# Second edge stage of a two-layer graph network: one-hot joins and accumulating scatters, or edges sorted by source with a scan and plain scatters

## Chip, cores and metric

One core of a Trainium2 chip. The metric is the device time of one execution in microseconds, of which the median over the runs is given. Everything is float32.

## The reference, cut to what matters

There are N = 100000 nodes with 64 features and E = 50000 edges (src, dst, weight), which come sorted by dst.

```python
# layer 0
agg = segment_sum(x[src] * w[:, None], dst, N)
out = leaky(x * agg @ W1 + b1) + leaky(agg @ W2 + b2)
x = layernorm(x + out * rsqrt(max(sum(out*out), 1e-12)))
# layer 1: the neighbour is dst, the sum goes to src
msg = gelu(gelu(x[dst] @ W1p + b1p) @ W2p + b2p) * w[:, None]
agg = segment_sum(msg, src, N)
h = gelu(gelu(concat(x, agg) @ W1u + b1u) @ W2u + b2u)
x = layernorm(x + h * rsqrt(max(sum(h*h), 1e-12)))
```

## The kernel before, in words

Three stages follow each other, with a barrier of all engines between them. Nodes go in 98 chunks of 1024 (128 partitions x 8), edges in 98 windows of 512 (4 tiles of 128).

**Stage one, `first_edges`.** For each window POOL gathers x[src] by four indirect DMAs (`gather`, L247) into xg, 120 of them ahead. PE spreads the window's 512 dst keys along the free axis (`spread_rows`, L292), DVE compares them with each tile's own keys, which gives matrices of 128 x 128 to 128 x 512 with the edge weight where the keys agree (`equal_rows`, L372, tile `weigh`), and counts with a second pass which edge of a run comes first (L378, tile `seen`). PE multiplies the matrices with the gathered rows (`join`, L304), so that one row of each run holds the run's sum; ACT copies it out (`take`, L327); POOL scatters the four tiles with accumulation into `table` in DRAM (`scatter`, L260), rows that are no run's sum going to spare rows. POOL issues a window's scatters only after those of the window before have landed. The first scatter is plain (bypass), and waits until `table` has been cleared, 25 transfers on SP's queue. Beside it SP loads chunks of x (`load_x`), DVE and ACT centre and copy them (`build`, L355 and L358; `copy_x`), and SP stores them next to the sums. DVE, PE and ACT work through a list `order` written out by hand, in which the entries (0, k) are the work above. The entries (1, k) do the same comparison for the second list of keys (src, with the edges still in order of dst): PE spreads, DVE compares and counts, and `store_join` on ACT's queue writes the window's matrices (640 KB) to `joins` in DRAM.

**Stage two, `second_edges`,** is a software pipeline of ROUNDS = NWIN + 6 rounds. In round t an engine does parts of windows t, t-1, ..., t-5, in the order written in its loop. One window is 12 blocks of 128 rows, 4 gathered for the edges (POOL, `gather`, L538, from `table` by dst) and 8 of the chunk (SP, `load`). Layer 0 is finished for all 12 (`box` is the input of a window, `y` its result), and layer 1's message is computed for the 4 edge blocks. The names of the steps, in the order of the engines' loops:

- PE: `products(t-2, 2)` (L588), `join(t-5)` (L634), `turn_neighbours(t-4)` (L607), `outputs(t-2, 0)` and `outputs(t-2, 1)` (L598, 12 matmul records each, one half of the bank pair o_p each), `first_product` (L614), `turn` and `products` 0 and 1 (L579, L588), `second_product(t-4)` (L619 bias, L621).
- ACT: `second_gelu` (L702), `slope(t-2, 2)` (L676), `take(t-5)` (L709), `square_centred` (L687), `neighbours_in`, `square(t-2)` (L682, from o_p to sq_o), then `evict` (L670), `first_gelu` and `slope` 0 and 1.
- DVE: `sum_outputs(t-2)` (L767), `roots` (L775 to L787, ten linked small operations), a copy of the root into the spare end of o_p (L789), `leak(t-1, 0)` (L758), `normalize(t-3)` (L806), `scale(t-2)` (L793, in place in PSUM), `leak` 1, `add_rows(t-2)` (L801), `leak` 2, three `multiply(t)` (L750), `sum_centred(t-2)` (L763).
- POOL: four scatters (L557, accumulating, into `state` by src), then the next gathers: on the average 359 / 91 a round.

The output block o_p is read last by `add_rows`, and `outputs(i, 0)` waits for `added` of the window before, for `squared` of it, and for `leak(i, 2)`. `join` multiplies the stored matrices, which SP loads (`load_join`, 640 KB), with the messages g2.

**Stage three, `last_rows`,** turns the node rows of `state` into the output.

## Time and profile before

| | |
|---|---|
| median of 3 runs | 2925.66 us (2924.0 to 2927.83) |
| the profiled execution, its own time | 2925.36 us |
| its span, first to last instruction | 2923.6 us |
| stage one, stage two, stage three | 0 to 1257, 1257 to 2539, 2539 to 2924 us |
| busy share of the span | POOL 80%, DVE 76%, PE 73%, ACT 36% |
| mean granted TensorE clock | 0.769 of full |

The span is a little shorter than the execution's time, since what lies ahead of the first instruction and behind the last is not in it. Engines run beside each other, so a busy share says how much an engine has to do, and an engine's idle time, with what ended it, says what it waited for. An operation that a row calls "issue" was waiting for nothing that the profile shows. A duration in a group is a mean; consecutive operations of one engine overlap by some hundredths of a microsecond.

### The profile page before, as it was taken

Reading aid. Unit: us, or ns where it says so; the run is one execution under the profiler, and the core shown is the slowest. Engines: PE = TensorE matmul, PEld = TensorE weight load, DVE = VectorE, ACT = ScalarE, POOL = GpSimd, SP = SyncE. Lnnn points to the kernel's source line nnn. Section 1 sums busy time; section 2 is a strip of 40 time slices with the busy share of each in tenths; the row PEclk is TensorE's granted clock in tenths of the full one; section 3 lists DMA queues with packets and bytes.
Section 4 is the critical chain, followed back from the end, with each engine's and each line's share of the span. In section 5 each row is a group of like instructions: output and inputs, shape, how many; then the busy total and the mean of one; then the engine's idle time right before and its main releaser. Section 6 shows DMA issues by size and latency. Waiting matters only on the chain. (4 is left out here: it accounts for less than half of the span.)

```text
span 2923.6 us, 40992 instructions
## 1 busy us (share of the span) xinstructions
PE 2133.4 (73%) x12594; PEld 1674.9 (57%) x12594; DVE 2219.9 (76%) x5824; ACT 1060.2 (36%) x1964; POOL 2327.0 (80%) x1770
## 2 busy tenths in 40 slices
PE   3036555555555553369999999999998999699997
PEld 3035555555555543347777777777776666466664
DVE  5069988888888886547788777777777777278998
ACT  0000000000000000035555555545554555289997
POOL 7777888888888888758878888888888887479998
PEclk8555555555555555579999999999999999699998
DMA  9889888888888767568777777777776776456664
GB/s 227 214 197 200 178 177 180 175 178 183 180 183 172 160 142 155 96 163 183 185 185 184 180 167 181 181 169 175 179 181 157 184 172 149 89 173 219 222 219 169
DMA packets 1035280, 516.39 MB, mean 177 GB/s; under 512 B 539713, under 2 KB 997489, under 8 KB 1035065
## 3 DMA queue, kind: packets, MB, share of 16 engines
q1 hardware_dynamic: 764616, 372.57, 48.1%
q0 software_dynamic: 143440, 76.97, 19.0%
q10 hardware_dynamic: 127008, 64.23, 7.6%
q8 instruction: 104, 1.70, 0.3%
q14 instruction: 112, 0.91, 0.1%
HBM read 269.84 MB, written 243.78 MB: 176 GB/s over the span
## 5 line engine op out<-in xcount | busy, mean ns | idle before, releaser
L304 PE MATMUL sums<-xg,weigh 128*128 128x64 f32 x1960 | 431.8, 416 | 518.2 <-ACT ms L327 350.9
L557 POOL DMA_INDIRECT state<-ms,sidx x391 | 621.5, 1590 | 147.4 <-issue 117.4
L304 PEld LDWEIGHTS sums<-xg,weigh 128*128 128x128 f32 x1960 | 417.6, 325 | 551.2 <-issue 474.9
L260 POOL DMA_INDIRECT table<-ms,sidx x391 | 615.7, 1575 | 136.1 <-issue 114.7
L372 DVE TENSOR_SCALAR weigh<-rowp,key,ew 128x128 f32<-128x128 f32 (+3 forms) x784 | 424.2, 604 | 162.8 <-PE rowp L292 155.4
L538 POOL DMA_INDIRECT box<-table,node_dst x391 | 385.8, 987 | 126.6 <-issue 111.2
L247 POOL DMA_INDIRECT xg<-in_x,node_src x391 | 380.8, 974 | 120.7 <-issue 107.1
L327 ACT ACTIVATE ms<-sums 128x256 f32<-128x256 f32 x98 | 37.6, 384 | 1137.9 <-DMA table<-ms,sidx 996.8
L378 DVE SCALAR_TENSOR_TENSOR seen<-rowp,key,earlier 128x128 f32<-128x128 f32 (+3 forms) x784 | 383.6, 546 | 0.0
L588 PE MATMUL z_p<-turned_s,wz 128*128 128x512 f32 x588 | 326.9, 639 | 22.7 <-ACT turned_s L670 21.0
L598 PE MATMUL o_p<-cenz,leaky 128*128 128x65 f32 x2352 | 302.1, 288 | 42.0 <-DVE leaky L758 41.9
L598 PEld LDWEIGHTS o_p<-cenz,leaky 128*128 128x128 f32 x2352 | 289.4, 203 | 62.8 <-DVE leaky L758 62.7
L292 PE MATMUL rowp<-ident,key 128*128 128x128 f32 x784 | 183.7, 413 | 130.1 <-DVE seen L378 123.1
L634 PEld LDWEIGHTS ffo<-g,weigh_in 128*128 128x128 f32 x1960 | 239.8, 196 | 48.1 <-issue 47.7
L676 ACT ACTIVATE leaky<-z_p,bz 128x512 f32<-128x512 f32 x294 | 202.0, 687 | 126.1 <-PE z_p L588 114.5
L767 DVE TENSOR_REDUCE v<-sq_o 128x12 f32<-128x780 f32 x98 | 94.6, 966 | 192.3 <-ACT sq_o L682 192.3
L292 PEld LDWEIGHTS rowp<-ident,key 128*128 128x128 f32 x784 | 164.4, 238 | 130.9 <-DVE seen L378 123.9
L634 PE MATMUL ffo<-g,weigh_in 128*128 128x64 f32 x1960 | 235.9, 277 | 1.6 <-issue 1.6
L758 DVE SCALAR_TENSOR_TENSOR leaky<-z_p,bz,leaky 128x512 f32<-128x512 f32 x294 | 218.5, 743 | 18.7 <-ACT leaky L676 9.1
L892 POOL TENSOR_TENSOR inv<-ssq,mhalf 128x8 f32<-128x8 f32 x98 | 161.0, 1642 | 59.1 <-DVE ssq L1004 59.1
L579 PEld LDWEIGHTS turned_p<-ident,box 128*128 128x128 f32 x1176 | 155.4, 153 | 84.6 <-issue 66.9
L670 ACT ACTIVATE turned_s<-turned_p 128x512 f32<-128x512 f32 x294 | 174.7, 595 | 47.4 <-PE turned_p L579 39.6
(97 smaller groups left out, 3555.2 us busy)
## 6 DMA issues: line engine op xcount, KB each, us to landing
box<-table SPq DMA_DIRECT2D x97, 768.0 KB, 5.2
joins<-weigh ACTq DMA_DIRECT2D x98, 640.0 KB, 3.8
weigh_in<-joins SPq DMA_DIRECT2D x98, 640.0 KB, 7.1
table<-rows SPq DMA_DIRECT2D x97, 512.0 KB, 5.3
pair<-state SPq DMA_DIRECT2D x97, 512.0 KB, 4.0
xin<-in_x SPq DMA_DIRECT2D x97, 256.0 KB, 6.1
state<-y SPq DMA_DIRECT2D x97, 256.0 KB, 7.5
out<-y SPq DMA_DIRECT2D x97, 256.0 KB, 2.2
```

The lines of the kernel that those rows point to most:

```text
L247: pool.indirect_dma_start(out=xg[:, i, :], out_offset=None, in_=x[:, :], in_offset=bass.IndirectOffsetOnAxis(ap=node[0][:, i:i + 1], axis= ...
L260: pool.indirect_dma_start(out=table[:, :], out_offset=bass.IndirectOffsetOnAxis(ap=sidx[0][:, i:i + 1], axis=0), in_=ms[k % MR][:, b, :], ...
L292: last = pe.transpose(rowp[n][k % 2][:, b * P:(b + 1) * P], key[n][:, i:i + 1].to_broadcast([P, P]), ident[:, :])
L304: last = pe.matmul(sums[k % 2][:, a * D:(a + 1) * D], block_of(0, k, b)[:, a * P:(a + 1) * P], xg[:, k * WT + b, :], start=b == a, stop=b ...
L372: last = dve.tensor_scalar(block_of(n, k, b), rowp[n][k % 2][:, (b + 1 - m) * P:(b + 1) * P], key[n][:, i:i + 1], ew[:, i:i + 1], ALU.is_e ...
L378: last = dve.scalar_tensor_tensor(out=seen[b][:, 0:m * P], in0=rowp[n][k % 2][:, (b + 1 - m) * P:(b + 1) * P], scalar=key[n][:, i:i + 1], ...
L538: pool.indirect_dma_start(out=box[i % SB][:, b, :, :].rearrange("p a f -> p (a f)"), out_offset=None, in_=table_rows[:, :], in_offset=bass ...
L557: pool.indirect_dma_start(out=state[:, :], out_offset=bass.IndirectOffsetOnAxis(ap=sidx[1][:, at:at + 1], axis=0), in_=ms[k % SM][:, b, :] ...
L588: pe.matmul(z_p[n % 2][:, :], wz[:, :], turned_s[q][:, :], start=True, stop=True).then_inc(z_up, 1)
L598: last = pe.matmul(o_p[:, b, g * M8:(g + 1) * M8], leaky[i % 2][r // 4][:, r % 4 * P:(r % 4 + 1) * P], cenz[:, :], start=True, stop=True)
L634: last = pe.matmul(ffo[:, (WT + a) * D:(WT + a + 1) * D], weigh[i % SW][:, at * P:(at + 1) * P], g2[i % 2][:, b * D:(b + 1) * D], start=b ...
L758: dve.scalar_tensor_tensor(out=leaky[i % 2][q][:, :], in0=z_p[n % 2][:, :], scalar=bz[:, 0:1], in1=leaky[i % 2][q][:, :], op0=ALU.add, op1 ...
```

## The change

Stage one no longer builds the second list's matrices. `equal_rows` becomes `weigh_rows` and `count_rows`, for the first list alone. Instead, the edges (src, dst, weight, as three float arrays `edges` of 128 x 512) are sorted by src with a bitonic network: 136 compare-and-swap steps, 16 changes of sign of a part of the keys, and 14 turns, which exchange the partition and the free axis by transposes on PE and copies on ACT. In a swap ACT copies the lower half of each pair aside (`keep_lower`), DVE compares the two halves' keys into a mask in PSUM, and makes two predicated copies. The 166 steps are spread over the windows: 12 each in windows 0 to 3, the others up to window 83. Then DVE marks which edge has the key of the one before and which ends a run, PE and ACT turn the lists once more, and the flags and the sorted weights (`runs`, 2 x 256 KB) go to DRAM.

Stage two gathers by the sorted dst. The messages stay transposed (features on partitions, one half of the edges on partitions 0 to 63 and the other on 64 to 127): `second_product` is one matmul and its bias goes into the Gelu. DVE multiplies them with the weights (`weight`) and forms running sums with `tensor_tensor_scan`, which begins anew where a run begins and carries on from window to window (`sum_runs`). PE turns the result back (`turn_back`), ACT takes it, and POOL scatters it without accumulation: rows that end no run go to spare rows of their own, and nothing waits for an earlier scatter. SP loads flags and weights of a window, each half broadcast over 64 partitions (256 KB in two transfers). One accumulating scatter at the end (`add_seam`) adds the run that crosses the two halves. `scale` now reads o_p and writes y in SBUF, straight behind `roots`, and `outputs` waits for `scaled` in place of `added`; `add_rows` and `normalize` work on y in SBUF, and the copy of the root into PSUM goes. The bound `FIRST, AT_ONCE, SORTED` is 4, 12, 84. On ACT `take(t-5)` moves behind `neighbours_in`.

The diff, cut to its core (the indentation is less than in the file):

```diff
+network = []
+turned_now, changes, turns = False, 1, 0
+for phase in range(1, PHASES + 1):
+    for bit in range(phase - 1, -1, -1):
+        if (bit >= LANES) != turned_now:
+            turned_now = not turned_now
+            network.append(("turn", phase, bit, changes, turns))
+            turns += 1
+        if bit == phase - 1:
+            network.append(("sign", phase, bit, changes, turns))
+            changes += 1
+        network.append(("swap", phase, bit, changes, turns))
+        changes += 1
+assert not turned_now
...
+FIRST, AT_ONCE, SORTED = 4, 12, 84
+def sorting(k):
+    def upto(r):
+        if r <= FIRST:
+            return min(AT_ONCE * r, len(network))
+        return min(len(network), AT_ONCE * FIRST + -(-(len(network) - AT_ONCE * FIRST) * (r - FIRST) // (SORTED - FIRST)))
+    return network[upto(k):upto(k + 1)]
...
-        for n, k in order:
-            if n == 1:
-                store_join(k)
-                continue
+        def keep_lower(phase, bit, done, before_it):
+            wait(act, arranged, done)
+            wait(act, laid, 3 * before_it)
+            act.activation(compact(lower[:, :, :], bit), pairs(edges[:, :, :], bit)[:, :, :, 0, :], ACT.Copy).then_inc(kept, 1)
+        def lay_edges(before_it):
+            for a in range(3):
+                n = 3 * before_it + a
+                act.wait_ge(spun, n + 1)
+                act.activation(edges[:, a, :], spun_p[n % 2][:, :], ACT.Copy).then_inc(laid, 1)
+        for k in range(NWIN):
+            for kind, phase, bit, done, before_it in sorting(k):
+                if kind == "swap":
+                    keep_lower(phase, bit, done, before_it)
+                if kind == "turn":
+                    lay_edges(before_it)
...
+        def compare(phase, bit, done, before_it):
+            wait(dve, arranged, done)
+            wait(dve, laid, 3 * before_it)
+            keys = pairs(edges[:, 0:1, :], bit)
+            dve.tensor_tensor(compact(above[:, 0:COLS // 2].bitcast(I32).rearrange("p (a c) -> p a c", a=1), bit)[:, 0, :, :],
+                              keys[:, 0, :, 0, :], keys[:, 0, :, 1, :], ALU.is_gt).then_inc(compared, 1)
+        def swap(phase, bit):
+            n = swap_number[phase, bit]
+            both, d = pairs(edges[:, :, :], bit), 1 << (bit - LANES if bit >= LANES else bit)
+            mask = compact(above[:, 0:COLS // 2].bitcast(I32).rearrange("p (a c) -> p a c", a=1), bit).to_broadcast([P, 3, COLS // 2 // d, d])
+            dve.wait_ge(compared, n + 1)
+            dve.wait_ge(kept, n + 1)
+            dve.copy_predicated(both[:, :, :, 0, :], mask, both[:, :, :, 1, :]).then_inc(lowered, 1)
+            dve.wait_ge(lowered, n + 1)
+            dve.copy_predicated(both[:, :, :, 1, :], mask, compact(lower[:, :, :], bit)).then_inc(arranged, 1)
...
+        for k in range(NWIN):
+            part = 0
+            for kind, phase, bit, done, before_it in sorting(k):
+                if kind == "sign":
+                    change_sign(phase, done, before_it)
+                if kind == "swap":
+                    compare(phase, bit, done, before_it)
+                    if part == 0:
+                        weigh_rows(k)
+                    if part == 1:
+                        count_rows(k)
+                        scatter_rows(k)
+                    part += 1
+                    swap(phase, bit)
+            if part < 1:
+                weigh_rows(k)
+            if part < 2:
+                count_rows(k)
                 scatter_rows(k)
-                if k < NCH:
-                    build(k)
+            if k < NCH:
+                build(k)
...
-        def load_join(i):
+        def load_runs(i):
             wait(sp, summed, i - SW + 1)
-            sp.dma_start(weigh[i % SW][:, :].rearrange("p (b f) -> p b f", f=P), joins[i].rearrange("b p f -> p b f")).then_inc(joined[i % SW], 16)
+            for h in range(2):
+                at = (HALF * h + 2 * i) * P
+                sp.dma_start(run[i % SW][h * D:(h + 1) * D, :, :],
+                             runs[:, at:at + 2 * P].rearrange("a (o f) -> o a f", o=1).to_broadcast([D, 2, 2 * P])
+                             ).then_inc(joined[i % SW], 16)
...
         def upto(k):
             return min(LEAD * WT + (FILLED - LEAD * WT) * k // (NWIN - 7), FILLED)
-        def scatter(k, h):
-            if h == 0:
-                pool.wait_ge(taken, k + 1)
-                wait(pool, scattered[HALVES - 1], 16 * JOIN * k)
-            else:
-                pool.wait_ge(scattered[h - 1], 16 * JOIN * (k + 1))
-            for b in range(JOIN * h, JOIN * (h + 1)):
-                at = k * WT + b
-                if at >= FILLED:
-                    break
-                pool.indirect_dma_start(out=state[:, :], out_offset=bass.IndirectOffsetOnAxis(ap=sidx[1][:, at:at + 1], axis=0),
-                                        in_=ms[k % SM][:, b, :], in_offset=None, compute_op=ALU.add,
-                                        engine_sem=begun if b == 0 else None).then_inc(scattered[h], 16)
+        def scatter(k):
+            pool.wait_ge(taken, k + 1)
+            for b in range(min(WT, FILLED - k * WT)):
+                of = column_of(HALF * (b % 2) + 2 * k + b // 2)
+                pool.indirect_dma_start(out=state[:, :],
+                                        out_offset=bass.IndirectOffsetOnAxis(ap=sorted_sidx[:, of:of + 1], axis=0),
+                                        in_=ms[k % SM][:, b, :], in_offset=None).then_inc(scattered[k % SM], 16)
+        def add_seam():
+            for s in range(SM):
+                missing = MISSING if (NWIN - 1) % SM == s else 0
+                pool.wait_ge(scattered[s], 16 * (WT * lies(NWIN, s, SM) - missing))
+            pool.indirect_dma_start(out=state[:, :], out_offset=bass.IndirectOffsetOnAxis(ap=seam_sidx[:, 0:1], axis=0),
+                                    in_=ms[(NWIN - 1) % SM][:, 2, :], in_offset=None, compute_op=ALU.add
+                                    ).then_inc(seamed, 16)
...
-                wait(pe, added, i)
+                wait(pe, scaled, i)
...
             pe.wait_ge(gelu1, i + 1)
-            wait(pe, gelu2, i)
-            pe.matmul(ffo[:, 0:WT * D], ones[:, :], bp2[:, :], start=True, stop=False)
-            for q in range(2):
-                last = pe.matmul(ffo[:, q * P:(q + 1) * P], g1[:, q * P:(q + 1) * P], wp2[:, :],
-                                 start=False, stop=q == 1)
-            last.then_inc(mixed2, 1)
-        def join(i):
-            pe.wait_ge(joined[i % SW], 16 * (i // SW + 1))
-            pe.wait_ge(gelu2, i + 1)
             wait(pe, taken, i)
-            for a in range(WT):
-                until = a // JOIN * JOIN + JOIN
-                for b in range(a, until):
-                    at = sum(SPAN[1][0:b]) + a % JOIN
-                    last = pe.matmul(ffo[:, (WT + a) * D:(WT + a + 1) * D], weigh[i % SW][:, at * P:(at + 1) * P],
-                                     g2[i % 2][:, b * D:(b + 1) * D], start=b == a, stop=b == until - 1)
-            last.then_inc(summed, 1)
+            pe.matmul(ffo[:, 0:2 * P], wp2[:, :], g1[:, :], start=True, stop=True).then_inc(mixed2, 1)
+        def turn_back(i):
+            pe.wait_ge(summed, i + 1)
+            wait(pe, taken, i)
+            for j in range(2):
+                last = pe.transpose(ffo[:, (2 + j) * P:(3 + j) * P], total[i % 2][:, j * P:(j + 1) * P], ident[:, :])
+            last.then_inc(turned_back, 1)
...
             of(t, 2, products, 2)
-            of(t, 5, join)
             of(t, 4, turn_neighbours)
             of(t, 2, outputs, 0)
+            of(t, 5, turn_back)
             of(t, 2, outputs, 1)
...
-            act.wait_ge(summed, i + 1)
-            for h in range(HALVES):
-                wait(act, scattered[h], 16 * JOIN * (i - SM + 1))
+            act.wait_ge(turned_back, i + 1)
+            wait(act, scattered[i % SM], 16 * WT * (i // SM))
...
         for t in range(ROUNDS):
             of(t, 5, second_gelu)
             of(t, 2, slope, 2)
-            of(t, 5, take)
             of(t, 3, square_centred)
             of(t, 4, neighbours_in)
+            of(t, 5, take)
             of(t, 2, square)
...
-            if q == 2:
-                wait(dve, begun, i - 4)
...
+        def weight(i):
+            dve.wait_ge(gelu2, i + 1)
+            dve.wait_ge(joined[i % SW], 32 * (i // SW + 1))
+            dve.tensor_tensor(g2[i % 2][:, :], g2[i % 2][:, :], run[i % SW][:, 1, :], ALU.mult).then_inc(weighted, 1)
+        def sum_runs(i):
+            dve.wait_ge(weighted, i + 1)
+            wait(dve, summed, i)
+            wait(dve, turned_back, i - 1)
+            dve.tensor_tensor_scan(total[i % 2][:, :], run[i % SW][:, 0, :], g2[i % 2][:, :],
+                                   total[(i - 1) % 2][:, 2 * P - 1:2 * P] if i else 0.0, ALU.mult, ALU.add).then_inc(summed, 1)
...
-            if t >= 3:
-                dve.tensor_scalar(o_p[:, 0, SPARE:SPARE + R], root[t % 2][:, 1, :], 1.0, None, ALU.mult).then_inc(spread, 1)
         def scale(i):
-            dve.tensor_tensor(banks(o_p, D), banks(o_p, D), halves(wide(root[i % 2][:, 0, :])), ALU.mult
-                              ).then_inc(scaled, 1)
-        def add_rows(i):
             s = i % SY
             wait(dve, stored[s], 16 * (i // SY))
             wait(dve, nt_up, i - SY + 1)
+            dve.tensor_tensor(halves(y[s][:, :, :]), banks(o_p, D), halves(wide(root[i % 2][:, 0, :])), ALU.mult
+                              ).then_inc(scaled, 1)
+        def add_rows(i):
+            s = i % SY
             dve.wait_ge(scaled, i + 1)
-            dve.tensor_tensor(halves(y[s][:, :, :]), banks(o_p, D), halves(box[i % SB][:, :, 2, :]), ALU.add).then_inc(added, 1)
+            dve.tensor_tensor(y[s][:, :, :], y[s][:, :, :], box[i % SB][:, :, 2, :], ALU.add).then_inc(added, 1)
         def normalize(i):
             s = i % SY
-            dve.wait_ge(spread, i + 1)
-            dve.tensor_tensor(y[s][:, :, :], y[s][:, :, :], wide(o_p[:, 0, SPARE:SPARE + R]), ALU.mult).then_inc(normed, 1)
+            dve.wait_ge(squared_y, i + 1)
+            dve.tensor_tensor(y[s][:, :, :], y[s][:, :, :], wide(root[(i + 3) % 2][:, 1, :]), ALU.mult).then_inc(normed, 1)
...
         for t in range(ROUNDS):
+            of(t, 5, weight)
+            of(t, 5, sum_runs)
             of(t, 2, sum_outputs)
             if 2 <= t < NWIN + 3:
                 roots(t)
+            of(t, 2, scale)
             of(t, 1, leak, 0)
             of(t, 3, normalize)
-            of(t, 2, scale)
             of(t, 1, leak, 1)
             of(t, 2, add_rows)
             of(t, 1, leak, 2)
```

## Rows read from the trace of the kernel before

**Rows 1.** Stretches: busy PE, PEld, DVE, ACT, POOL (xinstructions); granted clock, DMA share, GB/s.

```profile
300.00:600.00 300.00, 163.00 (x736) 152.96 (x735) 265.06 (x775) 24.45 (x54) 242.55 (x184) 0.51 0.84 178
...
1300.00:1600.00 300.00, 286.09 (x1786) 215.63 (x1785) 239.15 (x597) 163.68 (x298) 232.36 (x180) 0.99 0.78 182
...
1900.00:2200.00 300.00, 284.49 (x1696) 219.48 (x1694) 228.55 (x561) 154.10 (x281) 241.45 (x188) 0.93 0.74 173
```

**Rows 2.** Groups of instructions on POOL: busy and mean, then idle before.

```profile
L557 POOL DMA_INDIRECT state<-ms,sidx x391 | 621.5, 1590 | 147.4 <-issue 117.4
...
L260 POOL DMA_INDIRECT table<-ms,sidx x391 | 615.7, 1575 | 136.1 <-issue 114.7
...
L538 POOL DMA_INDIRECT box<-table,node_dst x391 | 385.8, 987 | 126.6 <-issue 111.2
```

**Rows 3.** Two lines: durations min/median/max, first and last start.

```profile
L260 POOL DMA_INDIRECT table<-ms,sidx x391: 968/1567/1642, 154.5 to 1254.2; - x196
...
L801 DVE TENSOR_TENSOR y<-o_p,box x98: 946/948/958, 1286.0 to 2503.8; 128x768 f32<-128x768 f32 x98
```

**Rows 4.** Timeline of DVE in one round of stage two: start, duration.

```profile
1701.50 0.74 DVE L758 SCALAR_TENSOR_TENSOR leaky<-z_p,bz,leaky 128x512 f32<-128x512 f32 x1
1702.15 1.09 DVE L750 TENSOR_TENSOR box<-box 128x256 f32<-128x256 f32 x3
1703.16 0.95 DVE L763 TENSOR_REDUCE v<-sq_y 128x12 f32<-128x768 f32 x1
1706.08 0.97 DVE L767 TENSOR_REDUCE v<-sq_o 128x12 f32<-128x780 f32 x1 [1.97 <-ACT sq_o L682]
...
1709.52 0.17 DVE L789 TENSOR_SCALAR o_p<-root 128x12 f32<-128x12 f32 x1
1709.60 0.74 DVE L758 SCALAR_TENSOR_TENSOR leaky<-z_p,bz,leaky 128x512 f32<-128x512 f32 x1
```

**Rows 5.** Timeline of PE, stage two, over four rounds.

```profile
1701.58 0.39 PE L607 MATMUL ffn<-ident,y 128*128 128x128 f32 x2
1702.29 2.89 PE L598 MATMUL o_p<-cenz,leaky 128*128 128x65 f32 x24 [0.32 <-DVE leaky L758]
...
1714.43 2.89 PE L598 MATMUL o_p<-cenz,leaky 128*128 128x65 f32 x24 [0.44 <-DVE leaky L758]
...
1727.09 4.67 PE L598 MATMUL o_p<-cenz,leaky 128*128 128x65 f32 x24 [1.03 <-DVE leaky L758]
...
1741.26 2.79 PE L598 MATMUL o_p<-cenz,leaky 128*128 128x65 f32 x24
```

**Rows 6.** Timeline of ACT in the same round as rows 4.

```profile
1705.22 0.82 ACT L682 ACTIVATE sq_o<-o_p 128x780 f32<-128x780 f32 x1 [2.05 <-PE o_p L598]
```

**Rows 7.** Groups by line and form, all stages, for the costs.

```profile
L372 DVE TENSOR_SCALAR weigh<-rowp,key,ew 128x128 f32<-128x128 f32 (+3 forms) x784 | 424.2, 604 | 162.8 <-PE rowp L292 155.4
L378 DVE SCALAR_TENSOR_TENSOR seen<-rowp,key,earlier 128x128 f32<-128x128 f32 (+3 forms) x784 | 383.6, 546 | 0.0
...
L292 PE MATMUL rowp<-ident,key 128*128 128x128 f32 x784 | 183.7, 413 | 130.1 <-DVE seen L378 123.1
...
L750 DVE TENSOR_TENSOR box<-box 128x256 f32<-128x256 f32 x294 | 106.7, 418 | 56.6 <-DMA box<-table,node_dst 56.6
...
L687 ACT ACTIVATE sq_y<-y 128x768 f32<-128x768 f32 x98 | 81.9, 836 | 1.4 <-DVE y L801 1.4
```

**Rows 8.** Waits: who waited for what, total, times, longest.

```profile
DVE means_p L355 <- DMA xin<-in_x: 112.1, 1, 112.1
```

**Rows 9.** DMA in the first 160 us: packets, then issues by line.

```profile
DMA packets 113095, 33.14 MB, mean 207 GB/s; under 512 B 107917, under 2 KB 111117, under 8 KB 113092
...
joins<-weigh ACTq DMA_DIRECT2D x2, 640.0 KB, 7.7
```

**Rows 10.** Timeline of POOL, windows 0 and 1 of stage one.

```profile
154.54 1.01 POOL L260 DMA_INDIRECT table<-ms,sidx  x1 [0.31 <-issue]
...
162.25 1.63 POOL L260 DMA_INDIRECT table<-ms,sidx  x1 [0.30 <-issue]
```

325 lines of the change are left out of this document (212 added, 113 removed).

## The prediction

> **What bounds the kernel now.** I read the busy time by stretch first, since three stages with different limits share one span [rows 1]. In the second stage POOL is busy 232 of 300 us, PE 286 and DVE 239, so no share alone tells the limit. POOL's groups do [rows 2]: an accumulating scatter takes 1590 ns and a gather 987, and nearly all of POOL's idle time is "issue", 0.3 us in front of each. Four scatters and, by the loop's rule, 3.9 gathers make 4 x 1.89 + 3.9 x 1.29 = 12.6 us a round, which is the pace measured: add_rows starts at 1286.0 the first and at 2503.8 the 98th time [rows 3], 12.55 us a round. POOL is the bound of stage two, and of stage one, where the same two kinds follow each other.
>
> Close behind lies a second limit, a loop through DVE, PE and ACT. From the end of leak 2 (1701.50 + 0.74, [rows 4]) PE runs the 24 matmuls of outputs, 2.89 us [rows 5], ACT squares them at 1705.22 for 0.82 [rows 6], and sum_outputs starts at 1706.08. DVE has three multiplies and sum_centred to fill this, and idles 1.97 us. After that it never stops until its next leak 2. This loop alone repeats in 12.01 us (its leak 0 at 1709.60, PE's next outputs at 1714.43). A change that relieves POOL is worth at most 12.55 - 12.0 a round unless it shortens this loop as well.
>
> **Part by part: stage one.** POOL's scatters, gathers and their order stay, and they set the pace of 11.3 us a window (1254.2 - 154.5 over 97, [rows 3]). What goes: the second list's half of weigh and seen on DVE, (424.2 + 383.6)/2/98 = 4.1 us a window [rows 7], its four transposes on PE, and 640 KB a window stored through ACT's queue. What comes is a sorting network of 136 swaps, 16 sign changes and 14 turns. A swap is one compare of 256 elements, like the multiply's 418 ns [rows 7], and two predicated copies of 768. No row shows such a copy; the nearest is a two-input operation of 768 elements, 948 ns [rows 3]. Nothing suggests half of that, and twice (1.9 us) is the other end. I take 0.95. ACT's copy of the lower half, 768 elements too, lies beside the compare and takes 836 ns [rows 7], so a swap is 2.4 to 2.9 us. A turn is 12 transposes of 183.7/784 = 0.23 us and ACT's copy behind the last, at most 0.84: 3.6 us.
>
> The first 48 steps (39 swaps, 9 signs) fall in windows 0 to 3: 39 x 2.9 + 4 x 5.9 + 2 = 139 us from 8 us on. DVE today waits 112.1 us there for an input chunk [rows 8], so they cost nothing. POOL starts to scatter at 154.5 with windows 0 to 2 and needs window 3 only 34 us later. The other 97 swaps, 7 signs and 14 turns spread over 80 windows: 1.21 x 2.6 + 0.18 x 3.6 = 3.8 us a window. DVE is busy 265 of 300 us [rows 1], 10.0 of 11.3; less 4.1 it has 5.4 free. ACT and PE have more. Cost zero; if that cover goes, DVE becomes the bound (a rival below). The first scatter waits for the clearing of the table, bound by DMA at 207 GB/s; two stores of 640 KB leave this stretch [rows 9], 1.3 MB, so 6 us less: **-6**. SP's four small new transfers wait for windows long done, and what is queued behind them has a chunk of slack: nothing.
>
> **Stage two, POOL.** The scatters become plain. Window 0 of stage one is plain already: 1.01 us for its first scatter against 1.63 for window 1's [rows 10], and the line's shortest is 968 ns [rows 3]. POOL then needs 4 x 1.28 + 3.9 x 1.29 = 10.2 us a round and no longer waits for the landing of its last window. It ceases to be the bound.
>
> **Stage two, PE.** The join of 20 matmuls goes, and the bias product; the second product is one matmul. About 3.5 us of PE leave, but none lies between leak 2 and sum_outputs, so none of it shortens the loop. In their place stand two transposes, turn_back, as long as turn_neighbours' 0.39 us [rows 5]. They are put between outputs 0 and outputs 1, and PE takes its work in order.
>
> **Stage two, DVE.** The copy of the root into PSUM goes (0.08 us, 1709.52 to 1709.60), and leak 2's wait for `begun`, which cost that round nothing. Scale, add_rows and normalize keep their 768 elements; SBUF or PSUM makes no row here differ. New are weight and the scan, 256 elements each, directly in front of sum_outputs. Weight is 0.42. The scan has no row: at least 0.42, at most 0.74, a 512-element operation (leak, [rows 4]), if each element costs two. I take 0.42, by its element count. The Trainium skill ("DVE: opcode table, instruction layouts, handler registers and perf-mode slots", section 6) says the built-in scan runs at half throughput. No row here shows a scan; by that page a round would be 0.27 us longer and the sum 26 us higher.
>
> **The step that decides.** turn_back of a window waits for its scan. After leak 2 DVE does the multiplies and sum_centred (1.87 us, 1702.24 to 1704.11, [rows 4]), weight (0.36 behind it), the link and the scan (0.46): 2.7 us. PE has finished outputs 0 at 1.5, half of 2.89, then stands until 2.75. turn_back ends at 3.15, outputs 1 at 4.55, the square and two hand-overs end at 5.45. Today sum_outputs starts 3.84 after leak 2. The loop grows by 1.6 - 0.08 to 13.55 us.
>
> **The clock.** Granted TensorE clock in stage two is 0.93 to 0.99 and 0.51 in stage one [rows 1], where PE is busy 55% of the time. One drop can be read off [rows 5]: after PE idled 1.03 us in front of 1727.09, the outputs took 4.67 instead of 2.89 us, half clock, and the next outputs came 14.17 us later instead of 12.14. In front of 1714.43 it idled 0.44 and kept the clock. The new round has PE idle about 1.2 us ahead of turn_back and, with the join gone, over 1 us ahead of outputs 0, and less matmul work besides. I expect a drop in nearly every round. Half of the outputs hides behind the scan, so it costs less than the 2.03 us of that round: 0.9 in outputs 1, 0.35 in turn_back, 0.1 in what follows. **The round becomes 14.9 us.**
>
> **The sum**, against the profiled execution's 2925.4 us (span 2923.6; the median of the runs, 2925.7, is the same): -6, + 97 x (14.9 - 12.55) = +228, + 6 for the last accumulating scatter of the seam (1.9 to issue; the landing, an estimate, about twice that), + 2 for POOL blocked now and then, = **3155 us**. Stage three is untouched. DMA's share falls (256 KB a window replace 640), which buys nothing, as no wait is for it. The two loads of runs are queued on SP behind a box load, 1.5 rounds before use.
>
> **Rivals.**
> 1. *Faster: the scan is no obstacle.* If scan and weight were done within outputs 0's 1.5 us, the loop would stay at 12.0: 97 x 0.55 = 53 us off, 2872 us; were sum_outputs' idle time filled too, POOL's 10.2 would decide and 2700 come out. It decides at the point where DVE needs less than 1.5 us from leak 2 to the scan's end. Against it: 1.87 us are spent before weight begins. 7%.
> 2. *The clock holds.* As computed, without the drops: 13.55, 2925.4 + 97 x 1.0 + 2 = 3024; with a 0.7 us scan 3050. For it: PE idled 0.44 without a drop, and no row tells where between that and 1.03 the edge lies. 22%.
> 3. *The sort is not hidden.* With predicated copies of 1.9 us a swap is 4.5: the first 48 steps end near 209 us, 21 after POOL needs window 3, and later windows need 6.1 of the 5.4 free, 0.7 x 80 = 56 us. On top of the forecast: 3155 + 77 = 3232. 14%.
> 4. *POOL is blocked in stage one*, where each delay counts. In stage two, with 1.09 us of operations with two SBUF inputs a round, a scatter takes 1590 ns, in stage one 1575 [rows 2], 15 ns for 9% of the time. The copies would cover 20%: 7 instructions x 0.09 x 84 windows = 53 us at most, as they are longer, 3208 us. The Trainium skill ("SBUF — State Buffer", section "Who interferes with whom") says that a DVE operation with two SBUF inputs contends only with a GpSimd instruction that reads SBUF; the 15 ns agree with a rare short wait. Against it speaks also that the copies' mask lies in PSUM. 4%.
> 5. *The plain scatters cost POOL as much as the accumulating ones.* POOL would need 12.6, still under 14.9: the forecast stands. Part of it.
>
> **The numbers.** Forecast 51%, rivals 7, 22, 14, 4, and 2% for a sum that happens to cancel. 0.2%, 6 us, is about what a measurement tells from no change. The range goes from 3015 (clock holds) to 3290 (the forecast with the slow scan and an unhidden sort); left out are rival 1, the cancelling case and longer stretches at half clock. Faster 0.07, same 0.02, slower 0.91.
>
> **What would show it.** DVE's idle time ahead of sum_outputs grows from 1.97 us to 2.7, and to 4 where the clock is halved; PE waits for the scan in turn_back, 98 times; L557's mean falls to 0.98 and POOL waits for ACT's take; the clock of stage two falls to 0.7 or 0.8; stage one keeps its length less 6 us. It is wrong if rounds are 12.5 us or less, if PE's turn_back never waits, or if stage one is longer.

## The result, and the profile after

The changed kernel takes **3156.65 us** (median of 4 runs, 3154.32 to 3158.42) against 2925.41 us before (4 runs, 2924.0 to 2927.83): ratio 1.0789, 95% interval 1.077 to 1.0808. It is slower by 231 us. The span of its profiled execution is 3155.7 us, against 2923.6.

Busy time by stretch, columns as in [rows 1] (PE, PEld, DVE, ACT, POOL, granted clock, DMA share, GB/s):

```profile
300.00:600.00 300.00, 152.46 (x724) 140.23 (x723) 239.24 (x526) 57.51 (x100) 244.38 (x183) 0.54 0.65 123
1300.00:1600.00 300.00, 240.91 (x986) 180.82 (x986) 211.59 (x495) 132.44 (x238) 157.76 (x151) 0.73 0.46 121
...
1900.00:2200.00 300.00, 242.54 (x988) 182.54 (x988) 209.38 (x494) 132.04 (x237) 164.00 (x158) 0.72 0.46 122
```

In stage one POOL is as busy as before, PE, DVE and DMA have less to do, and ACT has more (57.5 us instead of 24.5). In stage two every engine is less busy than before, and so is DMA, yet the stage is longer. That is the picture of a loop of waits, not of an engine at its limit. The granted clock has gone from 0.93 to 0.99 down to 0.72. The groups on POOL answer to [rows 2], L749 to L557, L325 to L260, L736 to L538:

```profile
L749 POOL DMA_INDIRECT state<-ms,sorted_sidx x391 | 378.7, 969 | 569.9 <-ACT ms L899 469.1
L325 POOL DMA_INDIRECT table<-ms,sidx x391 | 615.6, 1574 | 127.1 <-issue 117.1
...
L736 POOL DMA_INDIRECT box<-table,sorted_dst x391 | 439.0, 1123 | 128.3 <-issue 118.3
```

The plain scatter takes 969 ns where the accumulating one took 1590. That is 243 us less of POOL in stage two, and POOL now spends 469 us waiting for ACT to hand it messages. The two lines of [rows 3] give the lengths of the stages:

```profile
L1001 DVE TENSOR_TENSOR y<-y,box x98: 940/947/952, 1279.9 to 2745.4; 128x768 f32<-128x768 f32 x98
```

```profile
L325 POOL DMA_INDIRECT table<-ms,sidx x391: 969/1572/1735, 155.7 to 1247.3; - x196
```

A round of stage two is (2745.4 - 1279.9)/97 = **15.11 us**, from 12.55. The account of the 232 us between the two spans: up to the first add_rows 1279.9 instead of 1286.0, -6.1; 97 rounds of 2.56 us more, +247.7 (from the starts themselves); from the last add_rows to the end 410.3 instead of 419.8, -9.5.

One round on DVE, the counterpart of [rows 4] (L946 is the leak, L940 the multiply, L965 sum_centred, L953 the new weight, L960 the scan, L969 sum_outputs):

```profile
1900.88 0.75 DVE L960 TENSOR_TENSOR_SCAN total<-run,total,g 128x256 f32<-128x256 f32 x1
1905.72 0.97 DVE L969 TENSOR_REDUCE v<-sq_o 128x12 f32<-128x780 f32 x1 [4.09 <-ACT sq_o L873]
...
1913.04 0.74 DVE L946 SCALAR_TENSOR_TENSOR leaky<-z_p,bz,leaky 128x512 f32<-128x512 f32 x1
1913.70 1.09 DVE L940 TENSOR_TENSOR box<-box 128x256 f32<-128x256 f32 x3
1914.70 0.95 DVE L965 TENSOR_REDUCE v<-sq_y 128x12 f32<-128x768 f32 x1
1915.57 0.42 DVE L953 TENSOR_TENSOR g<-g,run 128x256 f32<-128x256 f32 x1
1916.02 0.75 DVE L960 TENSOR_TENSOR_SCAN total<-run,total,g 128x256 f32<-128x256 f32 x1
```

And the same two rounds on PE, the counterpart of [rows 5] (L798 is outputs, twice 12 records; L826 is turn_back):

```profile
1898.71 1.55 PE L798 MATMUL o_p<-cenz,leaky 128*128 128x65 f32 x12 [1.65 <-DVE leaky L946]
1901.69 0.69 PE L826 MATMUL ffo<-ident,total 128*128 128x128 f32 x2 [1.43 <-DVE total L960]
1902.17 2.66 PE L798 MATMUL o_p<-cenz,leaky 128*128 128x65 f32 x12
...
1913.84 2.70 PE L798 MATMUL o_p<-cenz,leaky 128*128 128x65 f32 x12 [1.65 <-DVE leaky L946]
1916.82 0.69 PE L826 MATMUL ffo<-ident,total 128*128 128x128 f32 x2 [0.29 <-DVE total L960]
1917.30 2.66 PE L798 MATMUL o_p<-cenz,leaky 128*128 128x65 f32 x12
```

Read the first round from the left. Outputs 0 needs 1.55 us, which is TensorE at its upper level of 2.4 GHz (granted clock 1.00 there), and then PE stands still for 1.43 us for the scan. Turn_back and outputs 1 come at the lower level of 1.2 GHz (granted clock 0.50): 2.66 us for the 12 records that outputs 0 ran in 1.55. In the second round outputs 0 is slow too (2.70 us) and the wait for the scan shrinks to 0.29. Over the 98 windows outputs 0 ran in 1.55 us 46 times, in the others in 1.8 to 2.8, and outputs 1 took more than 2.5 us 95 times. Either way outputs 1 ends some 6 us after leak 2. DVE meanwhile waits 4.09 us for the squares, against 1.97 before. Summed over the kernel, among the waits:

```profile
POOL state L749 <- ACT ms L899: 469.1, 94, 12.5
DVE v L969 <- ACT sq_o L873: 396.1, 98, 4.1
...
PE ffo L826 <- DVE total L960: 98.5, 97, 3.2
```

The wait of sum_outputs has doubled from 192.3 to 396.1 us, although DVE has 98 x 1.165 = 114 us of new work in front of it.

The new operations, by line (durations min/median/max, first and last start). Of the predicated copies of the sort and of the scan:

```profile
L530 DVE COPY_PREDICATED edges<-above,edges x136: 950/1008/1866, 10.9 to 1044.5; 128x768 f32<-128x768 int32 x136
```

```profile
L960 DVE TENSOR_TENSOR_SCAN total<-run,total,g x97: 750/751/752, 1323.7 to 2758.9; 128x256 f32<-128x256 f32 x97
L960 DVE TENSOR_TENSOR_SCAN total<-run,g x1: 691/691/691, 1308.6 to 1308.6; 128x256 f32<-128x256 f32 x1
```

The start of stage one, where the prediction had a term of -6. The timeline of POOL (L312 gathers, L325 scatters):

```profile
154.49 0.94 POOL L312 DMA_INDIRECT xg<-in_x,node_src  x1 [0.30 <-issue]
155.73 1.01 POOL L325 DMA_INDIRECT table<-ms,sidx  x1 [0.30 <-issue]
...
175.93 1.62 POOL L325 DMA_INDIRECT table<-ms,sidx  x1 [0.30 <-issue]
```

POOL issues its 120 gathers back to back, 1.25 us each, until 155.7, and its first scatter comes right behind them. It waits neither for the clearing of the table nor for the messages of window 0. Before it was the same, with the first scatter at 154.5. Window 2's messages, whose scatters start at 175.93, are taken out of PSUM by ACT (L419) at 168.32:

```profile
168.32 0.37 ACT L419 ACTIVATE ms<-sums 128x256 f32<-128x256 f32 x1
```

So the new work on DVE in these windows is hidden from POOL with some 7 us to spare.

### The profile page after: what moved, and what is told of

It reads as the page before. It is cut to its first block and busy times, and to the rows that moved or that the text cites. A ratio compares the mean times of both kernels' runs of the same rounds, so it can differ in the third digit from the quotient of the medians.

```text
span 3155.7 us, 36046 instructions
## 1 busy us (share of the span) xinstructions
PE 2119.5 (67%) x10223; PEld 1632.4 (52%) x10223; DVE 2319.4 (74%) x5189; ACT 1203.0 (38%) x2142; POOL 2141.8 (68%) x1774
## 5 line engine op out<-in xcount | busy, mean ns | idle before, releaser
L749 POOL DMA_INDIRECT state<-ms,sorted_sidx x391 | 378.7, 969 | 569.9 <-ACT ms L899 469.1
L325 POOL DMA_INDIRECT table<-ms,sidx x391 | 615.6, 1574 | 127.1 <-issue 117.1
L798 PE MATMUL o_p<-cenz,leaky 128*128 128x65 f32 x2352 | 453.0, 367 | 160.8 <-DVE leaky L946 160.8
L798 PEld LDWEIGHTS o_p<-cenz,leaky 128*128 128x128 f32 x2352 | 438.7, 284 | 185.3 <-DVE leaky L946 185.3
L736 POOL DMA_INDIRECT box<-table,sorted_dst x391 | 439.0, 1123 | 128.3 <-issue 118.3
L312 POOL DMA_INDIRECT xg<-in_x,node_src x391 | 383.2, 980 | 119.9 <-issue 106.7
L969 DVE TENSOR_REDUCE v<-sq_o 128x12 f32<-128x780 f32 x98 | 94.7, 966 | 396.1 <-ACT sq_o L873 396.1
L419 ACT ACTIVATE ms<-sums 128x256 f32<-128x256 f32 x98 | 37.5, 383 | 754.3 <-DMA table<-ms,sidx 710.9
L530 DVE COPY_PREDICATED edges<-above,edges 128x768 f32<-128x768 int32 x136 | 172.6, 1269 | 143.0 <-ACT lower L426 142.7
L467 DVE TENSOR_SCALAR weigh<-rowp,key,ew 128x128 f32<-128x128 f32 (+3 forms) x392 | 211.8, 603 | 75.3 <-PE rowp L358 75.3
L779 PE MATMUL turned_p<-ident,box 128*128 128x128 f32 x1176 | 245.9, 371 | 2.6 <-DVE box L940 2.6
L946 DVE SCALAR_TENSOR_TENSOR leaky<-z_p,bz,leaky 128x512 f32<-128x512 f32 x294 | 218.9, 745 | 8.0 <-ACT leaky L867 5.6
L426 ACT ACTIVATE lower<-edges 128x768 f32<-128x768 f32 x136 | 116.3, 855 | 219.7 <-DVE edges L532 176.6
L476 DVE SCALAR_TENSOR_TENSOR seen<-rowp,key,earlier 128x128 f32<-128x128 f32 (+3 forms) x392 | 191.4, 545 | 0.0
L532 DVE COPY_PREDICATED edges<-above,lower 128x768 f32<-128x768 int32 x136 | 172.9, 1271 | 4.7
```

What stands on the lines that cost most here:

```text
L312: pool.indirect_dma_start(out=xg[:, i, :], out_offset=None, in_=x[:, :], in_offset=bass.IndirectOffsetOnAxis(ap=node[0][:, i:i + 1], axis= ...
L325: pool.indirect_dma_start(out=table[:, :], out_offset=bass.IndirectOffsetOnAxis(ap=sidx[:, i:i + 1], axis=0), in_=ms[k % MR][:, b, :], in_ ...
L467: last = dve.tensor_scalar(block_of(k, b), rowp[k % 2][:, (b + 1 - m) * P:(b + 1) * P], key[:, i:i + 1], ew[:, i:i + 1], ALU.is_equal, ALU ...
L736: pool.indirect_dma_start(out=box[i % SB][:, b, :, :].rearrange("p a f -> p (a f)"), out_offset=None, in_=table_rows[:, :], in_offset=bass ...
L749: pool.indirect_dma_start(out=state[:, :], out_offset=bass.IndirectOffsetOnAxis(ap=sorted_sidx[:, of:of + 1], axis=0), in_=ms[k % SM][:, b ...
L779: last = pe.transpose(turned_p[n % 2][:, g * P:(g + 1) * P], box[i % SB][:, 4 * q + g, 0:2, :].rearrange("p a f -> p (a f)"), ident[:, :])
```

## The experiments

**How to compare them.** The experiments ran in three groups, each on a chip of its own. Beside the first and the third group the kernel before took 2991.29 and 2988.57 us, beside the second 2922.09, so the first and third ran on slower chips; the second is of the pace of the result's chip (2925.41). The changed kernel itself was run beside the second group, 3156.42 us, and beside the third, 3251.42, but not beside the first (turn_after, filled, mult_for_scan, added_wait). What ties the first group to the third is one kernel that ran in both, at 3248.99 us (added_wait) and 3248.84 us (added_wait_2). Only kernels on chips of the same pace are set against each other here, and the pace of stage two (first to last start of add_rows, over 97) is the number to compare:

| kernel | edit | time (us) | ratio, interval | round (us) | clock in stage two |
|---|---|---|---|---|---|
| *slower chips* | | | | | |
| changed_third | none | 3251.42 | 1.0888, 1.0847 to 1.0928 | 15.43 | 0.72 |
| turn_after | turn_back behind outputs 1 | 3064.11 | 1.025, 1.0195 to 1.0305 | 13.47 | 0.80 |
| filled | 7 unused matmuls a round | 3082.42 | 1.0309, 1.0254 to 1.0364 | 13.72 | 1.00 |
| mult_for_scan | product in place of the scan | 3221.28 | 1.0773, 1.0716 to 1.0831 | 15.07 | 0.73 |
| added_wait | outputs wait for added | 3248.99 | 1.087, 1.0811 to 1.0929 | 15.38 | 0.72 |
| added_wait_2 | the same | 3248.84 | 1.0877, 1.0834 to 1.0919 | 15.49 | 0.72 |
| copy_twice | more DVE work in the sort | 3296.01 | 1.1035, 1.0981 to 1.1088 | 15.47 | 0.72 |
| late_normalize | see below | 3004.17 | 1.0053, 1.0029 to 1.0077 | 12.90 | 0.99 |
| *chip as in the result* | | | | | |
| changed_again | none | 3156.42 | 1.08, 1.0782 to 1.0819 | 15.11 | 0.72 |
| turn_after_filled | turn_back behind outputs 1, 3 unused matmuls a round | **2859.9** | **0.9786, 0.977 to 0.9802** | 12.04 | 0.97 |
| turn_after_filled_add | and accumulating scatters | 2957.05 | 1.0113, 1.0096 to 1.0129 | 12.96 | 0.90 to 0.95 |
| filled_mult | filled, product for the scan | 2989.51 | 1.0228, 1.0211 to 1.0245 | 13.39 | 1.00 |

The two runs of the changed kernel itself, the controls:

> The changed kernel itself, as the measure for the other kernels of this call: the kernel before ran 2991 us beside the first four experiments, 2925 beside the change, so a round of stage two, not the whole time, is what can be carried over. Both theories: 15.1 us a round, ratio to the kernel before 1.08.

> The changed kernel once more, as the partner of the next run on the same chip. Theory and rival alike: a round of stage two at 15.1 us, 3156 us in all if the chip lands its transfers as the one of the profile before.

The first repeats the result to 0.3 us. The second shows a stage two of 15.43 us a round instead of 15.11, and with it the number that the runs on the slower chips have to be held against. Three kernels that should not differ there gave 15.38, 15.43 and 15.49, so a difference of 0.1 us between two of these rounds, each taken from one profiled execution, says nothing.

### turn_after: the place of turn_back

```diff
                             of(t, 2, outputs, 0)
-                            of(t, 5, turn_back)
                             of(t, 2, outputs, 1)
+                            of(t, 5, turn_back)
```

On ACT the take of the turned messages moves behind the square of the outputs in the same way.

> The changed kernel (3156.65 us, 15.1 us a round of stage two) with one thing moved: PE does turn_back after both halves of outputs, and ACT takes after its square. Theory, PE held by the scan between the halves: the outputs no longer wait for it, the idle time in turn_back's matmuls waiting for the scan nearly goes, and the round falls to 12.0 us where the clock holds (3156 - 97 x 3.1 = 2855 us), or to 14.3 where it still halves in each round, since 24 matmuls at half clock take 5.3 instead of 2.9 us (3078 us). Rival, the two added DVE operations (1.17 us) cost the time by themselves: the round stays within 0.3 us of 15.1, 3127 us or more.

The round falls from 15.43 to 13.47 us, by 1.96. In this the clock has a part: its granted share rose from 0.72 to 0.80. The wait for the scan is gone from PE's order: DVE's 84.9 us of delay to turn_back in changed_third are 4.5 us here. It didn't become 12.0, and PE's timeline says why:

```profile
1900.75 2.89 PE L798 MATMUL o_p<-cenz,leaky 128*128 128x65 f32 x24 [1.65 <-DVE leaky L946]
1903.74 0.44 PE L826 MATMUL ffo<-ident,total 128*128 128x128 f32 x2
...
1912.86 4.49 PE L798 MATMUL o_p<-cenz,leaky 128*128 128x65 f32 x24 [1.65 <-DVE leaky L946]
1917.15 0.63 PE L826 MATMUL ffo<-ident,total 128*128 128x128 f32 x2
...
1926.43 1.86 PE L798 MATMUL o_p<-cenz,leaky 128*128 128x65 f32 x12 [1.65 <-DVE leaky L946]
```

The two halves of the outputs follow each other without a gap. After PE has idled for 1.65 us they run in 2.89 us in one of these rounds and in 4.49 in the other, where the granted clock was 1.00 and 0.61; the first lasts 12.11 us and the second 13.57. The full clock is the rarer case: over the 98 windows both halves ran at it 22 times, and outputs 1 took more than 2.5 us 54 times. So more than half of what the change had added to a round comes back with the order on PE, and the order alone does not give back the rest of the clock.

### filled: the clock

Before outputs 0 three, and before turn_back four matmuls of the identity (120 columns) into a part of o_p that nobody reads, `o_p[:, 1, 392:512]`:

```diff
+                            of(t, 2, fill, 3)
                             of(t, 2, outputs, 0)
+                            of(t, 2, fill, 4)
                             of(t, 5, turn_back)
```

> The changed kernel with unused matmuls into spare columns of the output block where PE idles: three ahead of outputs 0 and four ahead of turn_back, about 0.25 us each at full clock. Theory, PE's idle stretches halve its clock in each round: granted clock of stage two rises from 0.72 to over 0.9 and the round falls from 15.1 to 13.9 us (13.55 as forecast for the full clock, plus 0.33 for the scan's true length), 3156 - 97 x 1.2 = 3040 us. Rival, the clock is held down by something else or is not on the path: the time stays at 3157 us, or grows by the matmuls put in, 3157 to 3300 us.

The round is 13.72 us, and the stretch of 1700 to 2000 us shows the clock at its upper level throughout:

```profile
1700.00:2000.00 300.00, 227.32 (x1395) 169.54 (x1394) 232.05 (x547) 145.95 (x263) 168.37 (x175) 1.00 0.50 134
```

PE is given more to do and is busy for less time, 227 of 300 us instead of 238 in the same stretch of changed_third, with 1395 matmul records against 962. Holding the clock is thus worth 15.43 - 13.72 = 1.7 us a round on this kind of chip. Some 0.3 us of them seem to belong to the chip: between 1400 and 2300 us DVE's leaks stand idle for 18.4 us in changed_third, 0.32 us a round, for 1.3 us in changed_again on the other kind of chip, and for 0.0 in filled. Set beside the 15.11 us of the other kind, the clock is worth 1.4 us. The round of 13.72 is close to what the prediction worked out for the loop without drops (13.55).

### turn_after_filled: both

Three filling matmuls stand before outputs 0, and turn_back comes behind outputs 1.

> turn_back behind both halves of outputs and the unused matmuls ahead of outputs 0, both together. Theory, the place of turn_back and the clock are all that lengthened the round: the loop is back at the 12.0 us of the kernel before (0.08 less for the root's copy), POOL's plain scatters need only 10.2, so the ratio to the kernel before falls to 0.98: 97 x (15.1 - 12.0) = 300 us less than the changed kernel. Rival, something else of the change costs time too: the round stays above 12.6 us, ratio 1.00 or more.

Round 12.04 us, 2859.9 us in all, 62 us less than the kernel before on the same chip. The timeline of DVE shows sum_outputs waiting 0.85 us instead of 4.09. PE's shows the filling (six records for three matmuls) and the outputs in one piece at full clock:

```profile
1909.94 0.75 DVE L966 TENSOR_TENSOR_SCAN total<-run,total,g 128x256 f32<-128x256 f32 x1
1911.55 0.97 DVE L975 TENSOR_REDUCE v<-sq_o 128x12 f32<-128x780 f32 x1 [0.85 <-ACT sq_o L879]
```

```profile
1905.95 0.83 PE L832 MATMUL o_p<-ident 128*128 128x120 f32 x6
1907.76 2.89 PE L798 MATMUL o_p<-cenz,leaky 128*128 128x65 f32 x24 [0.98 <-DVE leaky L952]
1910.75 0.44 PE L826 MATMUL ffo<-ident,total 128*128 128x128 f32 x2
```

Sum_outputs starts 3.85 us after the end of leak 2 (1906.96 + 0.74), against 3.84 before. This is the old loop of 12.01 us, unhindered by POOL and with weight and scan placed in DVE's former idle time. The two edits save 3.07 us a round together on this chip. Against the -1.96 and -1.71 that each saves alone on the slower chips they overlap.

### turn_after_filled_add: what the plain scatters are worth

```diff
-                                                        in_=ms[k % SM][:, b, :], in_offset=None).then_inc(scattered[k % SM], 16)
+                                                        in_=ms[k % SM][:, b, :], in_offset=None, compute_op=ALU.add).then_inc(scattered[k % SM], 16)
```

> The kernel turn_after_filled with the four scatters accumulating again (the rows are distinct, so none waits for another). Theory, POOL's time matters as soon as the loop is 12.0 us: 4 x 1.88 + 3.9 x 1.28 = 12.5 us a round, about 50 us more than turn_after_filled. Rival, it is the wait for the landing of the window before that made POOL the bound, not the duration: within 10 us of turn_after_filled.

2957.05 us, 97 more than with plain scatters, nearly twice what was expected. The round is 12.96 us, and nearly all of POOL's idle time is "issue" again. Its scatter:

```profile
L749 POOL DMA_INDIRECT state<-ms,sorted_sidx x391 | 641.6, 1641 | 137.5 <-issue 117.9 <-ACT ms L905 19.5
```

4 x (1.64 + 0.3) + 3.9 x (1.04 + 0.3) = 13.0 us a round, from this row and the gathers' mean of 1038 ns there. By the durations of [rows 2] it would have been 12.6 us, some 50 us more in all; 50 ns more for each of eight transfers is the rest. The result for the change: the plain scatters, which sorting the edges allows, are worth 0.9 us a round, 88 us in stage two, to a kernel whose other loop is at 12.04. In the changed kernel, at 15.11, POOL's 13.0 us would not bind, so none of it should be seen; that was not run.

### mult_for_scan and filled_mult: the price of the scan

The scan is replaced by a plain product of the same two operands, so the running sums are left out.

```diff
-        dve.tensor_tensor_scan(total[i % 2][:, :], run[i % SW][:, 0, :], g2[i % 2][:, :],
-                               total[(i - 1) % 2][:, 2 * P - 1:2 * P] if i else 0.0, ALU.mult, ALU.add).then_inc(summed, 1)
+        dve.tensor_tensor(total[i % 2][:, :], run[i % SW][:, 0, :], g2[i % 2][:, :], ALU.mult).then_inc(summed, 1)
```

> The changed kernel with the scan (0.75 us) replaced by a plain product of the same two inputs (about 0.41 us), so that runs are not summed. Theory, the scan lies in full on the path from leak 2 to sum_outputs: 0.34 us a round less, 97 x 0.34 = 33 us, 3124 us. Rival, PE is late anyway at half clock (outputs 0 takes 2.7 us then and ends near the scan's end): half of it or less, 3140 to 3157 us.

Set beside the 15.11 us of the changed kernel, 15.07 looked like nothing saved. But 15.11 is another chip's number. Against the changed kernel on its own kind of chip (15.43) it saves **0.36 us a round**, and 30 us in all. Against added_wait, which ran beside it on the same chip and is worth as much as the changed kernel (see below), it is 0.31 us and 28 us. The scan is longer than the product by 0.751 - 0.41 = 0.34. Within the 0.1 us that two such rounds differ anyway, the whole of it is on the path, also at the low clock.

> The kernel filled (full clock, turn_back still between the halves, 13.72 us a round) with the scan replaced by a plain product of 0.41 us. Theory: at full clock PE waits for the scan (0.49 us idle after the unused matmuls), so the 0.34 us come off in full, 13.4 us a round, 33 us less than filled. Rival, the scan is not on the path: 13.7.

It gave 13.39 us a round, 0.33 less than filled. Filled ran on the slower kind of chip only, where the changed kernel's round is longer by just as much (0.32), so the pair alone decides nothing. The traces speak for the scan: the idle time of DVE's leaks, in which the chips differ for the changed kernel, is 0.0 us in both, and PE's wait for the scan ahead of turn_back is 0.49 us in filled and 0.16 to 0.17 here. The run shows one thing more. It is the very loop that the prediction worked out for the full clock, with a scan of 0.42 us, on the result's kind of chip: 13.39 us where 13.55 were forecast.

### added_wait and added_wait_2: the release of the output block

```diff
-                                wait(pe, scaled, i)
+                                wait(pe, added, i)
```

> The changed kernel with outputs waiting for add_rows of the window before again, as the kernel before did, in place of scale. Theory: no change, 3157 us within 4, because outputs 0 also waits for leak 2, which DVE does after add_rows, so the block's release never binds. Rival, the early release of the output block is worth time: scale ends some 3 us ahead of add_rows, and the round grows by up to that, 3250 us or more.

> The outputs wait for the sum with the residual again, as before the change, instead of for the scaling out of PSUM. Theory, that freeing the block one operation earlier is worth nothing because TensorE asks for it long after both: the round stays at 15.11 us and the time within 4 us of the changed kernel on this chip. Rival, that the first reading on another chip (15.38 us a round) was the edit and not the chip: 15.38 us again, 97 x 0.27 = 26 us more.

The first reading, 3248.99 us, seemed to cost 90 us until the changed kernel itself was run on that kind of chip: 3251.42 against 3248.84 us, rounds of 15.43 and 15.49, beside each other on one chip. **Freeing the block at scale instead of at add_rows is worth nothing.** The rows of PE above say why: outputs 0 starts at 1913.84, after leak 2, and in DVE's order leak 2 comes behind both scale and add_rows. A buffer that is free before the last operand is there is never waited for.

### copy_twice: is the sort hidden?

The second predicated copy of each swap is made twice, 136 copies more. (The expectation speaks of some 28 a window; that is a slip, it is 136 over the whole of stage one.)

```diff
                             dve.copy_predicated(both[:, :, :, 0, :], mask, both[:, :, :, 1, :]).then_inc(lowered, 1)
-                            dve.wait_ge(lowered, n + 1)
+                            dve.wait_ge(lowered, 2 * n + 1)
+                            dve.copy_predicated(both[:, :, :, 1, :], mask, compact(lower[:, :, :], bit)).then_inc(lowered, 1)
+                            dve.wait_ge(lowered, 2 * n + 2)
```

> In stage one the second predicated copy of every swap runs twice, some 28 more copies of about 1.1 us a window of nodes sorted, so the sort costs VectorE about a third more; stage two is as it was. Theory, that the sort lies wholly in VectorE's idle time beside a GpSimd stage: the last scatter of stage one stays at 1247 us and the time at 3156, within 5. Rival, that it is hidden only just: the window of stage one grows by what VectorE lacks, the last scatter comes 30 us later or more, 3190 or more in all.

3296.01 us, 45 more than changed_third. The last scatter of stage one starts at 1335.9 instead of 1296.0 us, but where the 40 us lie matters. POOL's timeline of copy_twice:

```profile
199.07 1.63 POOL L325 DMA_INDIRECT table<-ms,sidx  x1 [36.46 <-ACT ms L419]
256.52 1.62 POOL L325 DMA_INDIRECT table<-ms,sidx  x1 [46.34 <-ACT ms L419]
```

and of changed_third:

```profile
223.19 1.62 POOL L325 DMA_INDIRECT table<-ms,sidx  x1 [48.32 <-ACT ms L419]
```

With the extra copies POOL waits 82.8 us for windows 1 and 2, without them 48.3 us for window 2 (on this chip; on the chip of the result it waits for neither). These are the windows in which 12 steps each are done. Behind them it makes no difference: from 500 to 1000 us POOL is busy 403.8 us in copy_twice and 407.1 in changed_third, while DVE goes from 398 to 470 of 500. So both sides were half right. At 1.2 swaps a window the sort is hidden, with room for a third more; in windows 0 to 3 it is hidden only while the rest of the start is on time. On the slower chips POOL does wait there, and most of their 49 us in stage one (1296.0 against 1247.3) is this one wait. The extra copies lengthen it by 34.5 us, so there they are on the path; whether the sort as it is would cause the wait by itself, or something else makes the start late, was not tracked down; PE waits for something that the trace does not name, 51.2 us at a time.

### late_normalize: filling the last idle time

The kernel turn_after_filled, with DVE's normalize moved from between leak 0 and leak 1 to ahead of the next round's sum_outputs. It isn't the only thing moved. PE does turn_neighbours behind turn_back instead of ahead of the filling, and first_product behind products 0; ACT does neighbours_in behind evict 0 and first_gelu behind slope 0; and there is a fourth filling matmul. DVE's part:

```diff
                             of(t, 5, sum_runs)
+                            of(t, 4, normalize)
                             of(t, 2, sum_outputs)
...
                             of(t, 1, leak, 0)
-                            of(t, 3, normalize)
                             of(t, 1, leak, 1)
```

> The kernel with turn_back behind both halves of the outputs and with the filling matmuls (2859.9 us, round 12.04), and the last multiply of a window (normalize) moved from behind the scaling of the next window to ahead of its sum_outputs, into the 0.85 to 1.15 us for which VectorE waits there for the squares of the outputs; what depends on it moves one round later. Theory, that this wait is idle time that other work can fill: a round of 12.04 - 0.85 = 11.2 us, 97 x 0.85 = 82 us less, 2778. Rival one, that the outputs are then late in turn because TensorE waits for leak 2 and ScalarE's squares for it: half of that or less, 11.6 or more, 2820 or more. Rival two, that GpSimd (1.18 + 3 issue gaps + 4 x 0.97 us a round) takes the bound: 11.5 or more.

A miss: the round is 12.90 us and the ratio to the kernel before 1.0053, against 0.9786 without the move. turn_after_filled wasn't run on this chip; the changed kernel is slower there by 0.9% of the ratio, which does not cover 2.7. From the timelines of DVE, PE and ACT in one round:

```profile
1909.86 0.75 DVE L952 SCALAR_TENSOR_TENSOR leaky<-z_p,bz,leaky 128x512 f32<-128x512 f32 x1 [0.48 <-ACT leaky L873]
...
1915.64 0.97 DVE L975 TENSOR_REDUCE v<-sq_o 128x12 f32<-128x780 f32 x1 [1.16 <-ACT sq_o L879]
```

```profile
1910.66 2.89 PE L798 MATMUL o_p<-cenz,leaky 128*128 128x65 f32 x24 [0.68 <-DVE leaky L952]
```

```profile
1914.79 0.82 ACT L879 ACTIVATE sq_o<-o_p 128x780 f32<-128x780 f32 x1 [4.24 <-PE o_p L798]
```

and ACT's square in turn_after_filled, whose outputs end at 1907.76 + 2.89:

```profile
1910.69 0.82 ACT L879 ACTIVATE sq_o<-o_p 128x780 f32<-128x780 f32 x1 [2.50 <-PE o_p L798]
```

Normalize now stands in the time behind the scan, but sum_outputs still waits 1.16 us. One part of the reason is on DVE. PE makes the third product only after leak 0 has freed its block, then ACT's slope and DVE's leak 2 follow, and normalize between leak 0 and leak 1 had covered some of that: with it gone leak 2 waits 0.48 us. That alone would still leave a gain, and the part of the round from the start of sum_outputs to the end of the next leak 2 did get shorter, from 8.16 to 7.88 us in the mean of windows 10 to 89.

The loss lies in the other part, from leak 2 to sum_outputs, which grew from 3.90 to 5.10 us. PE ends the outputs at 1913.55, and ACT starts to square them 1.24 us later, with nothing else running on ACT since 1910.55. In turn_after_filled that step is 0.04 us in every window; here it is more than 0.5 us in 87 of 98, with a median of 1.26. What holds ACT back the trace does not name, and as operations on PE and ACT were moved together with normalize, the run doesn't tell which move did it. The cause stays open. It isn't POOL (rival two), which waits 313 us for ACT's messages. So the miss does not show that this idle time can't be filled, only that this arrangement loses more than it fills.

## Why the prediction came out right

3155 us were forecast and 3156.65 measured. That closeness is partly luck; by its own steps:

- **Stage one is bound by POOL, the sort costs nothing.** Shown. POOL's pace is 11.25 us a window ((1247.3 - 155.7)/97), against 11.34. A swap costs DVE more than taken, though: the predicated copies take 1.27 us in the mean, not 0.95. They come in two kinds, told apart by the order of the swaps: 1.84 to 1.88 us where the elements lie in pieces of one or two next to each other (44 swaps), 0.95 to 1.02 where the pieces have four or more (92 swaps). 136 x 2 x 0.32 = 87 us more than planned went into idle time. Rival 3 (the sort is not hidden), at 14%, comes true in the first windows of copy_twice, with half as many copies again, on a slower chip.
- **-6 for the clearing of the table.** The size came out (the first add_rows is 6.1 us earlier), the reason did not. The step took the first scatter as waiting for DMA. It follows POOL's 120 gathers, and is even 1.2 us later than before. Stage one is shorter because POOL's waits for ACT's messages in front of its scatters fell from 12.8 to 1.6 us. DMA was the busiest resource of that stretch (busy share 0.91 in the first 150 us), and I took it for the releaser, although POOL's own row says "issue" [rows 10].
- **POOL ceases to be the bound of stage two.** Shown: 969 ns a scatter, against 0.98 forecast. That alone brings nothing. turn_after_filled and its partner with accumulating scatters show what it is worth when the loop lets it through.
- **turn_back between the outputs' halves.** Shown by turn_after: 1.96 us a round, with what it gives back of the clock. The wait was forecast at 1.2 us at full clock; it is 1.43 where outputs 0 ran at full clock and 0.29 where it didn't.
- **The scan at 0.42.** Mis-sized. It takes 0.751 us for 256 elements, 1.8 times the weight's 0.414. The Trainium skill ("DVE: opcode table, instruction layouts, handler registers and perf-mode slots", section 6) says that the built-in scan runs at half throughput; the trace agrees. mult_for_scan shows that the 0.34 us by which it is longer than a product are on the path.
- **The clock falls in nearly every round.** Shown: 0.72 granted, outputs 1 over 2.5 us in 95 of 98 windows, and the round that filled gives back. For the size, the result's kind of chip counts: from 13.39 us (filled_mult) and 0.34 for the scan the loop at full clock is 13.73 us, and 15.11 - 13.73 = 1.38 is the clock, an estimate from these runs, where 1.35 were forecast. So of the 0.21 us by which the round came out above 14.9, the scan is +0.34, the clock +0.03, and the loop at full clock -0.16 (13.39 instead of 13.55). Rival 2 (the clock holds) would have given 3024 or 3050 us, and filled, where it does hold, comes near: 3082 us on the slower chip, or 1.0309 of the kernel before, 3016 on the other.
- **+6 for the seam, +2 for POOL.** The seam is about right, the end of stage two came out with the other sign. The part behind the last add_rows is 9.5 us shorter. Before, POOL ran behind: its last scatter started at 2535.5, 31.7 us after the last add_rows, because it was the bound and had a backlog. Now it starts at 2763.8, 18.4 us after, which is 13.3 less; some 4 us come back, with the seam's scatter, which starts 2.9 us later and lands in 3.2. I had priced the operation that is added and not the backlog that goes with a bound.
- **The release of the output block**, of which the prediction expected nothing: shown to be worth nothing by added_wait_2.

The sum, term by term, has +248 for the rounds where +228 was forecast, and -16 at the two ends where +2 was. The two errors, +20 and -18, cancel to 2 us, and that is luck; inside the +20 the scan's +33 and the loop's -16 also lie against each other. The upper end of the range, 3290, does not follow from what is named for it: 3155 + 26 for the slow scan + 77 for the unhidden sort are 3258.
